# Moving the shared expert into the routing stage and scatter-adding the expert results

## What is computed

```python
h = rmsnorm(layernorm(x2), norm_w)                      # residual = layernorm(x2)
scores = softmax(h @ router_w.T)                        # 32 experts
topk_w, topk_ids = top_k(scores, 4); topk_w /= topk_w.sum(-1)
g, u = split(ragged_dot(h[tok_idx], w1, group_sizes))   # w1: 512 x 2*256 per expert
ys = ragged_dot(silu(g) * u, w2, group_sizes)           # w2: 256 x 512 per expert
routed = sum_k(ys of the token's k-th expert * topk_w[k])
shared = silu(h @ sg) * (h @ su) @ sd                   # 512 x 512 each, every token
out = x2 + layernorm(residual + routed + shared)
```

## Time and profile before

| | us |
|---|---|
| median of 3 runs (4079.18 to 4085.52) | 4080.21 |
| span of the profiled execution | 4079.6 |
| attention | 2693.7 |
| dispatch | 129.6 |
| experts | 837.6 |
| finish | 418.7 |

### The profile page before, as it was taken

One profiled execution on the slowest core, in us unless ns is written; L12 is line 12 of the kernel. 1 busy time (PEld: TensorE's weight loads), 2 busy tenths in 40 slices (PEclk: granted clock), 3 DMA queues, 4 the chain that ended last, 5 costly groups with the idle time before them and its releaser, 6 DMA issues. The chain is left out here.

```text
span 4079.6 us, 72707 instructions
## 1 busy us (share of the span) xinstructions
PE 3524.6 (86%) x20387; PEld 2980.0 (73%) x20389; DVE 2461.7 (60%) x5012; ACT 1655.2 (41%) x3410; POOL 1188.8 (29%) x1594
## 2 busy tenths in 40 slices
PE   6999995999997899999599999725999899988886
PEld 5888885888886788888588888623777677766665
DVE  6666666666666666666666666677444444436666
ACT  2444352444443244344243443310555555543333
POOL 2333330333332133333133333331212122223332
PEclk9999996999998799999699999955999999989999
DMA  1000002001002000000200000132444554444444
GB/s 52 28 17 15 25 22 89 14 15 28 17 15 81 27 28 14 15 27 17 94 14 15 28 14 15 56 117 70 154 154 145 164 159 148 157 157 146 146 145 126
DMA packets 169472, 282.14 MB, mean 69 GB/s; under 512 B 12880, under 2 KB 65488, under 8 KB 169136
## 3 DMA queue, kind: packets, MB, share of 16 engines
q1 hardware_dynamic: 115664, 143.27, 10.5%
q0 software_dynamic: 23120, 75.78, 6.7%
q10 hardware_dynamic: 30352, 58.99, 4.4%
HBM read 210.62 MB, written 67.37 MB: 68 GB/s over the span
## 5 line engine op out<-in xcount | busy, mean ns | idle before, releaser
L422 DVE TENSOR_TENSOR ptl<-TP,pth 128x512 fp32r<-128x512 f32 (+1 forms) x640 | 407.6, 637 | 280.4 <-ACT pth L558 270.1
L558 ACT CAST pth<-TP 128x512 fp32r<-128x512 f32 (+1 forms) x640 | 349.2, 546 | 298.8 <-PE TP L694 296.7
L611 PE MATMUL O<-pth,vh 128*128 128x256 f32 (+1 forms) x1280 | 400.2, 313 | 22.9 <-DVE ptl L422 22.9
L280 POOL TENSOR_SCALAR oTh<-onorm 128x256 fp32r<-128x256 f32 x256 | 104.2, 407 | 999.5 <-DVE onorm L428 999.5
L410 DVE TENSOR_REDUCE negmax<-S 128x1 f32<-128x384 f32 (+7 forms) x512 | 381.7, 747 | 15.6 <-PE S L679 10.5
L611 PE MATMUL S<-wph,xTh 128*128 128x512 f32 (+1 forms) x1024 | 354.7, 346 | 7.0 <-DVE xTl L367 6.6
L613 PE MATMUL O<-pth,vl 128*128 128x256 f32 (+1 forms) x1280 | 359.5, 281 | 0.0
L612 PE MATMUL O<-ptl,vh 128*128 128x256 f32 (+1 forms) x1280 | 358.3, 280 | 0.0
L612 PE MATMUL S<-wpl,xTh 128*128 128x512 f32 (+1 forms) x1024 | 347.4, 339 | 0.0
L272 POOL TENSOR_TENSOR work<-work,cst 128x320 f32<-128x320 f32 x128 | 132.9, 1038 | 736.2 <-ACT work L542 736.2
L613 PE MATMUL S<-wph,xTl 128*128 128x512 f32 (+1 forms) x1024 | 345.8, 338 | 0.0
(11 more groups left out here) (240 smaller groups left out, 9301.6 us busy)
## 6 DMA issues: line engine op xcount, KB each, us to landing
y_d<-yb SPq DMA_DIRECT2D x145, 256.0 KB, 3.2
raww<-in_L_ffn_w_dram ACTq DMA_DIRECT2D x32, 1024.0 KB, 6.6
prob<-in_L_attn_x_dram SPq DMA_DIRECT2D x9, 2048.0 KB, 9.4
stage<-in_L_attn_w_aq_dram SPq DMA_DIRECT2D x68, 256.0 KB, 2.8
stage<-in_L_attn_w_ao_dram SPq DMA_DIRECT2D x64, 256.0 KB, 2.6
raww<-in_L_ffn_w_dram ACTq DMA_DIRECT2D x32, 512.0 KB, 8.3
x<-x_d SPq DMA_DIRECT2D x34, 256.0 KB, 4.4
hb<-h_d ACTq DMA_DIRECT2D x33, 256.0 KB, 2.6
```

What stands on the lines that cost most here:

```text
L280: nc.gpsimd.tensor_scalar(slot(oTh, u), onorm[:], 1.0, 1.0, ALU.mult, ALU.mult).then_inc(o_hi, 1)
L422: nc.vector.tensor_tensor(ptl[:, n % 2, 0:w], TP[:, n % 2, 0:w], pth[:, n % 2, 0:w].bitcast(F32), ALU.subtract).then_inc(tp_lo, 1)
L558: nc.scalar.copy(pth[:, n % 2, 0:w], TP[:, n % 2, 0:w]).then_inc(tp_hi, 1)
L611: mm(out, ah, bh, start=first, stop=False)
```

## The change

The stages become attention, `route`, experts and finish.

**route** does the dispatch's work and, between its steps, 24 of the 32 shared tiles (`NS = 24`), fully unrolled. All four engines follow an order written out by hand. The result of each tile, residual plus shared, is stored to a new accumulator `acc_d` in DRAM; for tiles 24 to 31 the residual alone. The gates are spread into a dense [token, expert] table that is stored behind each row of `h_d`, whose rows grow from 512 to 544 elements. The blank stores go; a spare tile behind `h_d` and `acc_d` takes the empty slots. The first expert is split here.

**experts** gathers the longer rows, reads the tile's expert and takes its gate column, and multiplies the gate into the activation. A result is no longer stored to `y_d` but added to `acc_d` by an indirect DMA with an addition, each of which waits for the one before it.

**finish** has 8 shared tiles, and for all 32 loads the accumulator and x2 through eight buffers, takes statistics, normalises and adds. The root is a power on GpSimd.

The diff, cut to its core. First the sizes, attention's store of h, and SP's order in `route`:

```diff
+HW = M + E
+NS = 24
-                sp.dma_start(h_d[b].rearrange("(t p) m -> p t m", p=P), work[:]).then_inc(stored, 16)
+                sp.dma_start(h_d[bass.ds(b * T, T), 0:M].rearrange("(t p) m -> p t m", p=P), work[:]).then_inc(stored, 16)
...
+            for i in range(NTILE):
+                s = i % 2
+                if i + 2 < NS:
+                    sp.wait_ge(t_done, i + 1)
+                    sp.dma_start(hb[:, s], h_t[i + 2, :, 0:M]).then_inc(h_in[s], 16)
+                sp.wait_ge(ob_ready, i + 1)
+                sp.dma_start(acc_t[i], ob[:, s]).then_inc(out_stored[s], 16)
+                if i + 2 < NTILE:
+                    sp.dma_start(xb[:, s], x2_t[i + 2]).then_inc(x_in[s], 16)
+                if i == 8:
+                    sp.wait_ge(slots_ready, 1)
+                    for e in range(2):
+                        load_expert(sp, raww, e, w1[e], w2[e], experts_in[e])
+            sp.wait_ge(dense_ready, 1)
+            sp.dma_start(h_d[0:NTOK, M:HW].rearrange("(t p) m -> p t m", p=P), dense[:]).then_inc(dense_out, 16)
+            sp.wait_ge(blanked, 32)
+            sp.wait_ge(dense_out, 16)
+            sp.wait_ge(experts_in[1], 32)
+            for s in range(2):
+                sp.wait_ge(out_stored[s], 16 * (NTILE // 2))
```

GpSimd's order in `route`:

```diff
+            def plain(i):
...
+                s = i % 2
+                pool.wait_ge(x_in[s], 16 * (i // 2 + 1))
+                if i >= 2:
+                    pool.wait_ge(out_stored[s], 16 * (i // 2))
+                dst = (xb if i < NS else ob)[:, s]
+                nc.gpsimd.tensor_scalar(dst, xb[:, s], negm[:, i:i + 1], coef[:, i, K + 1:K + 2],
+                                        ALU.add, ALU.mult).then_inc(xn_ready if i < NS else ob_ready, 1)
+            def with_shared(i):
+                s = i % 2
+                pool.wait_ge(xn_ready, i + 1)
+                pool.wait_ge(o_read, i + 1)
+                nc.gpsimd.tensor_tensor(ob[:, s], xb[:, s], osb[:, s], ALU.add).then_inc(ob_ready, 1)
...
+            pool.wait_ge(negm_ready, 1)
+            for i in range(2):
+                plain(i)
+                with_shared(i)
+            pool.wait_ge(g_ready, 1)
+            for k in range(K):
+                dst = dense if k == 0 else part
+                if k >= 2:
+                    pool.wait_ge(d_step, 2 * k - 1)
+                nc.gpsimd.tensor_tensor(dst[:], hot[:, k].bitcast(F32), coef[:, :, k:k + 1].to_broadcast([P, NTILE, E]), ALU.mult).then_inc(d_step, 1)
+                if k >= 1:
+                    pool.wait_ge(d_step, 2 * k)
+                    nc.gpsimd.tensor_tensor(dense[:], dense[:], part[:], ALU.add).then_inc(d_step if k < K - 1 else dense_ready, 1)
+            for i in range(2, NTILE):
+                plain(i)
+                if i < NS:
+                    with_shared(i)
+            pool.wait_ge(e_hi, 1)
+            nc.gpsimd.tensor_tensor(wel[:, 0], raww[:, 0], weh[:, 0].bitcast(F32), ALU.subtract).then_inc(e_lo, 1)
```

VectorE's order in `route`. `lo_h(i)` and `lo_act(i)` make `hTl` and `aTl` of tile i, `gated(i)` makes `ac`; `front(i)` is `lo_h(i + 1)` and then `lo_act(i - 1)`; the others are the parts of the former dispatch:

```diff
+            which()
+            totals()
+            gates()
+            lo_h(0)
             cum = prefix(tot, (cumA, cumB), NTILE, lambda x, a, b: x[:, a:b])
+            front(0)
+            places(cum)
+            ends = tiles(cum)
+            gated(0)
+            even(ends)
+            front(1)
+            owners(ends)
+            gated(1)
+            front(2)
+            tables(ends)
+            gated(2)
+            spread()
+            front(3)
+            masked()
+            gated(3)
+            front(4)
+            slots()
+            gated(4)
+            rows()
+            picked = 0
+            for i in range(5, NS):
+                front(i)
+                for _ in range(2 if picked + 2 <= NTILE else 0):
+                    select(picked)
+                    picked += 1
+                gated(i)
+            lo_act(NS - 1)
+            for i in range(picked, NTILE):
+                select(i)
+            listing()
```

ScalarE's order in `route` (`hi_h` makes `hTh`), and PE's:

```diff
+            def result(i):
+                s = i % 2
+                act.wait_ge(dn_done, i + 1)
+                if i >= 2:
+                    act.wait_ge(ob_ready, i - 1)
+                nc.scalar.copy(osb[:, s], O[:]).then_inc(o_read, 1)
+            for i in range(NS):
+                if i + 1 < NS:
+                    hi_h(i + 1)
+                if i >= 1:
+                    act.wait_ge(at_done, i)
+                    nc.scalar.copy(flatten(aTh), TP[:, 1]).then_inc(ah_done, 1)
+                act.wait_ge(gu_done, i + 1)
+                nc.scalar.activation(sl[:], S[:, 0], ACT.Silu).then_inc(silu_done, 1)
+                if i >= 1:
+                    result(i - 1)
+            act.wait_ge(at_done, NS)
+            nc.scalar.copy(flatten(aTh), TP[:, 1]).then_inc(ah_done, 1)
+            act.wait_ge(experts_in[0], 32)
+            nc.scalar.copy(weh[:, 0], raww[:, 0]).then_inc(e_hi, 1)
+            result(NS - 1)
+            def transpose_h(i):
+                pe.wait_ge(h_in[i % 2], 16 * (i // 2 + 1))
+                if i >= 1:
+                    pe.wait_ge(hl_done, i)
+                for c in range(MC):
+                    ins = nc.tensor.transpose(TP[:, 0, c * P:(c + 1) * P], hb[:, i % 2, c * P:(c + 1) * P], ident)
+                ins.then_inc(t_done, 1)
...
+            def down(i):
+                pe.wait_ge(al_done, i + 1)
+                if i == 0:
+                    pe.wait_ge(w_lo, 3 * MC)
+                else:
+                    pe.wait_ge(o_read, i)
...
+            for i in range(NS):
+                if i + 1 < NS:
+                    transpose_h(i + 1)
+                if i >= 1:
+                    transpose_act(i - 1)
+                gate_up(i)
+                if i >= 1:
+                    down(i - 1)
+                if i == 5:
+                    pe.wait_ge(sel_ready, 1)
+                    mm(I[:, 0:XW], zero[:, 0:P], zero[:], start=True, stop=False).then_inc(listed, 1)
+                if i >= 5 and picked + 2 <= NTILE:
+                    list_rows(picked)
+                    list_rows(picked + 1)
+                    picked += 2
+            transpose_act(NS - 1)
+            down(NS - 1)
+            for i in range(picked, NTILE):
+                list_rows(i)
```

The experts, first on GpSimd, then ScalarE's `result` and VectorE:

```diff
+            def scatter(t, s, landed, count):
+                if landed is not None:
+                    landed_apart(pool, y_out[1 - s], landed)
+                pool.sem_inc(y_free, 1)
+                nc.gpsimd.tensor_copy(idy[:, s:s + 1], ids[:, bass.ds(t, 1)]).then_inc(idy_ready, 1)
+                wait_apart(pool, idy_ready, count)
+                wait_apart(pool, y_ready, count)
+                nc.gpsimd.indirect_dma_start(acc_d, bass.IndirectOffsetOnAxis(ap=idy[:, s:s + 1], axis=0), yb[:, s], None,
+                                             compute_op=ALU.add).then_inc(y_out[s], 16)
...
+            with pool.Fori(1, before) as j:
+                for s in range(2):
+                    t = pool.snap(j * 2 + s)
+                    wait_apart(pool, hl_done, t + 3)
+                    gather(pool.snap(t + 4), s, t + 5)
+                    scatter(t, s, (j + s) * 16, t + 2)
...
             def result(n):
                 wait_apart(act, dn_done, n + 1)
                 act.wait_ge(y_free, n + 1)
-                nc.scalar.copy(yb[:, n % 2, :], O[:]).then_inc(y_ready, 1)
+                nc.scalar.copy(yb[:, (n + 1) % 2, :], O[:]).then_inc(y_ready, 1)
...
+            def gate_of(t, s):
+                at = v.snap(v.to_reg(s * HW + M + expert_of(v, t)), min_val=M, max_val=2 * HW - 1)
+                nc.vector.tensor_copy(gcol[:], xgf[:, bass.ds(at, 1)]).then_inc(g_ready, 1)
...
+                        wait_apart(v, g_ready, t + 1)
                         v.wait_ge(silu_done, t + 1)
-                        nc.vector.tensor_tensor(ac[:], sl[:], S[:, FI:2 * FI], ALU.mult).then_inc(act_ready, 1)
+                        nc.vector.scalar_tensor_tensor(out=ac[:], in0=S[:, FI:2 * FI], scalar=gcol[:], in1=sl[:],
+                                                       op0=ALU.mult, op1=ALU.mult).then_inc(act_ready, 1)
+                        v.wait_ge(hh_done, t + 2)
+                        v.wait_ge(act_ready, t + 1)
+                        nxt = v.snap(v.to_reg(t + 1), min_val=1, max_val=XT)
+                        gate_of(nxt, v.snap(nxt % 2))
                         lo_h(t + 1)
```

The finish: the order of the tiles, SP's loads, and VectorE's order, in which `sums(n)` adds the shared result where there is one (one pass), and makes statistics, and `close(n)` normalises and adds x2:

```diff
+NH = NTILE - NS
+GROUPS = [[3 * i, 3 * i + 1, 3 * i + 2] + ([NS + i - 2] if i >= 2 else []) for i in range(NH)] + [[NTILE - 2], [NTILE - 1]]
+ORDER = [i for group in GROUPS for i in group]
...
+                i, s = ORDER[n], n % NL
+                for dst, src in ((a0, acc_t), (x2, x2_t)):
+                    sp.dma_start(dst[:, s], src[i]).then_inc(a_in[s], 16)
+            for n in range(NTILE):
+                if n % 3 == 0 and n // 3 + 2 < NH:
+                    i = n // 3
+                    sp.wait_ge(t_done, i + 1)
+                    sp.dma_start(hb[:, i % 2], h_t[NS + i + 2, :, 0:M]).then_inc(h_in[i % 2], 16)
```

(74 more changed lines are left out.)

602 lines of the change are left out of this document (314 added, 288 removed).

## The result

The changed kernel takes 4281.07 us (median of 4 runs) beside 4079.69 us of the kernel before on the same chip: 1.0493 times as long, 95% interval 1.0474 to 1.0513. The forecast was 4351. The profiled execution spans 4283.1 us, 203.5 more than before; the working is judged against that.

A forecast was written before the change was run, and what follows sets the result against it. VectorE was taken to bound the dispatch, PE the experts, and VectorE's waits for x2 and weighing the finish. Finish -290, dispatch +372, experts' start and end -7, expert tiles +196 gave +271 on 4079.6: 4351 us, range 4215 to 4490.

The forecast's parts named there:

- Finish, -290: Finish: VectorE bounds it at 129 us against 418.7, as 5 start, 93 plain tiles, 24 shared tiles, 7 tail.
- Dispatch, +372: Dispatch: exposed h load makes each section 18.3 us, twenty-one periods 384; 501 us in all, bounds +310 to +430.
- The two one-offs: Dispatch: tile 2's result waits for dense gates on GpSimd, 5 us; expert weights go ahead of an h, 8.
- rival (b): Dispatch: h load not exposed because PE has other work; period 10.6 us, total 4191; chance 0.09.
- Experts, the gate: Experts: value load and copy on VectorE between hTh and hTl cost 1.25 us; alone 5.63 becomes 6.63 per tile.
- L: Experts: time from an adding scatter's issue to its landing, taken as 5.2 us.
- S: Experts: scatter chain's period per tile, hand-off 1.25 us plus L, taken as 6.45 us (5.55 to 8.15).
- rival (a): Experts: scatter chain alone decides, landing 6.9 us, period 8.15, +360 in place of +196, total 4515; chance 0.15.
- by the formula with doubled bytes: Experts: by the skill page's DMA formula the scatter lands in 4.2 us and its chain is hidden, leaving the gate alone.
- Two chains: Experts: gate at 6.63 and scatter at 6.45 together give 6.85 us; clock adds 0.15, period 7.0, +196.
- (c): Dispatch load not exposed, gate read beside other work, expert period stays 5.63: 3995 us; chance 0.06 with a better finish.
- (d): Experts: gate cheap (0.9 - 0.25), scatter hidden, clock as now: 4248 us; chance 0.13.

The follow-up runs named there:

- e6_all: Changed kernel with h asked for one tile earlier, the gate read behind aTl, two accumulators and four y buffers, whole computation: 4042.5 us.
- e1_h_ahead: Changed kernel with SP asking for h of tile i+3 before waiting for tile i's result in the dispatch: 4145.5 us.
- e9_fixed_column: Changed kernel with the gate's column fixed, without the value load, one accumulator and two y buffers kept: 4304.6 us.
- e4_two_chains: Changed kernel with even and odd tiles adding into two accumulators and four y buffers, gate left in place: 4250.1 us.

## Why the prediction was right or wrong

**Direction, and the place of the loss: right.** Finish gained what was forecast, the dispatch lost most, by the mechanism named, and the experts the rest. The time lies 70 us under the forecast and inside its range, but the experts' share came by another mechanism than the forecast's, see below. Of the 67.5 us by which the sum was too large on the span, 38 are the dispatch's and 36 the experts' tiles', and the experts' start and end take 8 of them back.

**Finish, -290: right in sum, not in its parts.** VectorE was to be over 80% busy; it is 68% (87.85 of 129.0). A plain tile takes less than the 2.9 us that I took from the earlier trace rows. I let the next tile's statistics cover 0.5 us of the 3.4 between the first statistics and the end of the last pass; they cover 1.1, the waits between the small steps and the reciprocal too:

```profile
4202.86 0.69 DVE L1634 BATCH_NORM_STATS2 stat<-a 128x6 f32<-128x512 f32 x1
...
4205.11 0.69 DVE L1634 BATCH_NORM_STATS2 stat<-a 128x6 f32<-128x512 f32 x1
```

2.25 us, so 72 for 32 tiles and not 93. The shared tiles take it back: VectorE's waits show 44.6 us for hTh in 8 times, of which 23.7 is its idle time across the end of the experts. The two errors cancel. The loads don't bound it: 8.4 MB more in e6_all cost 5.5 us.

**Dispatch, +372 against +333.8: mechanism right, term by term a little large.** The gap is 6.19 (6.8), the PE work with its slow start 10.90 (9.5 + 2), the period 17.09 (18.3): 25 us of the error are here. Landing after issue was 3.12 (3.4). down(0) ended near 2743 (2750), the last section and down took 13.8 (17), the tail from there 25.7 (31). The two one-offs were 3.9 and 9.6 (5 and 8), from the stores at 2762.98, 2783.93, 2886.29 and 2912.91. The e1_h_ahead run shows cause and price together, and rival (b): 323 us with the load hidden. Its 10.16 against my 10.6 and 4146 against 4191 differ by these small terms and those of the experts.

**Experts, start and end: start right, end missed.** The second gate/up comes 16.1 us into the stage (27.3 before), a gain of 11.2 where I wrote 10. The end is 16.1 after PE's last down matmul, where it was 4.3 and I added 3: y of the last two tiles wait in the chain, 4137.17 and then 4143.18, and the finish starts 10.95 after the last issue. The landing takes 4.9 of that. Then GpSimd's sequencer spends 5.46 us in the DRAIN that closes the stage, and all engines wait for it:

```profile
L1264 POOLq DRAIN  x1: 5457/5457/5457, 4148.4 to 4148.4; - x1
```

In the kernel before it took 2.69 us and was over before the last store had landed; the forecast has no term for it. Why it lasts twice as long here no run shows.

**Experts, the gate: size nearly right, its effect wrong.** The gap was 1.31 us (1.25). Alone it makes 5.60 into 6.48 silu to silu, +0.88, where I had +1.00. The Trainium skill, "DMA: Bandwidth & Descriptors", Latency and other measured facts, has a floor of about 600 ns for a tensor_load; it was 310 ns here (338 in the earlier trace rows), and the measurement decides.

**Experts, the scatter: the step that failed.** I took L = 5.2 and 1.25 of hand-off, S = 6.45. The median landing is 5.16, the hand-off 1.00. But one scatter in five lands late, 29 of 143, by (5.73 - 5.16) x 143/29 = 2.8 us on average. I named the weight loads as a disturbance and gave them no term of the sum. They are 0.63 us a tile, and with them the chain by itself takes 6.82, above the gate's 6.48. So rival (a)'s mechanism holds for the mean (the scatter chain needs the whole time with the gate gone), at 6.72 in place of its 8.15, and taking the gate's read away gains nothing. Against (a) the prediction says that plain landings are stable. The kernel before shows otherwise. For its 144 gathers from 2844 us on (L1039) the trace has

```profile
DMA to landing us min/median/max: 3.2/3.7/6.8
```

26 of them take over 5 us. The one at 2872.47, 3.5 us behind a weight load's issue, takes 6.5, and the mean of all is 4.13. So the missing term could be estimated from the kernel before: 0.4 us a tile by the gathers, mean less median.

The Trainium skill, "DMA: Bandwidth & Descriptors", Anatomy of one DMA, has 2.0 us and the bytes over 436 GB/s, an estimate of 2.6 us here. A plain scatter comes near (2.98 at the fifth percentile), an adding one takes 4.9 or more, even with no weight loads, so "by the formula with doubled bytes" was no guide.

**Two chains "give more than either": wrong.** 6.45 and 6.63 were to give 6.85. In fact 6.82 (chain, e9_fixed_column) and 6.48 (gate, e4_two_chains) give 6.72, no more than the longer one alone; neither did the clock fall (0.97, 0.96 before), for which I had put 0.15. An S that was too short and a combination that was too dear left 7.0 where 6.76 was measured in the same count: 36 us of the error.

**Rivals (c) and (d)** didn't come to pass. What (c) asked for, h asked for in time and the gate beside other work, needed a third thing that it left out, a scatter chain with room: then 4042.5 is reached, against its 3995.

## What to carry to other kernels

A DMA that each one of its kind waits for is a serial chain, and it competes with the work as a whole by its mean: median landing, hand-off, and the late ones that other loads on the chip cause. Price these late ones as a term; the landings of a similar DMA in the kernel before show them, if one reads their mean and longest and not only the median. Where two chains run side by side, shortening the shorter brings nothing and can hide what the longer costs, so test each with the other out of the way. And when a queue's list puts a load behind the wait for a result, look whether that load is the first thing the next section needs: here moving it by one line of the list gave back 136 of 201 us.

## What the runs showed of the hardware

- An adding indirect DMA of 128 rows of 2 KB holds GpSimd for 1.61 us, and GpSimd goes on 4.9 to 5.2 us after its issue; an overwriting one holds it for 1.01 and takes 2.98 (fifth percentile).
- Beside a 1.5 MB weight load, issued from 4.3 us ahead of it to 1.3 behind, 29 of 143 adding scatters took 6.2 to 9.2 us; overwriting scatters (5.9 and more) and gathers (up to 6.8) were late there too.
- In the dispatch, a pause of 5.17 us was followed by transposes at twice their time (1.12 against 0.61 us for four). The work behind it took 1.58 us more (granted clock 0.85 against 1.00).
- GpSimd's DRAIN at the end of a stage took 5.46 us behind the last scatter; in the kernel before it took 2.69.
